# Products of y ahead of the up half of gated block 3, and the rest of M ahead of VectorE's product for up block 2, in a fused delta-rule and gated-MLP kernel

## The chip, the cores and the metric

The kernel runs on one core of one Trainium2 chip. The metric is the device time of one execution in microseconds (us), lower is better. The engines are named as the profile names them: PE is TensorE's matmul, PEld its weight load (which runs beside the matmuls), DVE is VectorE, ACT is ScalarE, POOL is GpSimd, SP is SyncE, which here only issues DMAs.

## The reference, cut to what matters

There are 32 sequences of T = 512 tokens with C = 256 channels. For each of them:

```
x  = x + attn(_layernorm(x))
x  = x + ffn(_layernorm(x))
# attn: layernorm, then delta
#   q, k, v = split(x @ gates_w + gates_b);  k normalised
#   A = tril(k k^T, -1) + I;   u = solve_triangular(A, v)
#   y = (q k^T) (lr * u);      delta = y @ out_w + out_b
#   x = x + delta;   x = x + relu(layernorm(x) @ w1 + b1) @ w2 + b2
# ffn:  h = silu(x @ w_gate^T) * (x @ w_up^T)   (768 hidden);   h @ w_down^T
```

Since q k^T times a matrix can be bracketed the other way, the kernel does not form the 512 x 512 score. It collects one C x C matrix for each sequence, multiplies it by the weights on both sides, and calls the result M. The attention output of the 512 tokens is then one product of the normalised tokens with M. That product is "y" here.

## The kernel before, in words

**Arithmetic.** Most products are made with pairs: an operand is kept as a high part and a rest (`_hi`, `_lo`, tensor type fp32r), and a product is three matmuls (hi by hi, hi by lo, lo by hi; `split_matmul`, L166 to 177). A rest is made by `dve_rest` (L1506), which subtracts the high part, written by ScalarE, from the whole. The gate and up products use the exact integer weights, and so two matmuls (high part and rest of the tokens) for each of the two blocks of 128 channels: four matmuls of 512 columns each for a half of one block.

**Stages.** After a setup phase over all sequences (some 280 us in the profile), a loop over i runs three sequences at once, skewed by one step: the attention part of sequence i (`att`), the MLP and the gate and up halves of sequence i-1 (`mlp`), and the down product of sequence i-2 (`down`). `overlapped` (L988) calls each engine's body with i = 0 to 33. att runs for i = 0 to 31, mlp for i = 1 to 32. Both are there for i = 1 to 31, that is in 31 iterations.

**Order of the work.** Nothing schedules: each engine has its own body, written out by hand (`pe_body` L1155, `act_body` L1341, `dve_body` L1551, `pool_body` L1682, `sp_body` L1782), and runs its instructions in that order. The engines meet only at semaphores (`wait_ge`, and `after`, L984, which waits only when the count is above zero).

**The steps around the change,** in the order of one iteration:

- The gated MLP has six blocks of 128 hidden channels, h = 0 to 5. `pe_gate_up(pe, i, h)` (L1090 to 1111) makes the gate half into PSUM bank FG and then the up half into bank FU (h even) or S0 (h odd). The gate half waits until ScalarE has read the gate half of block h-1 (`sg_ev[h-1]`). The up half waits until VectorE has read the up half of block h-2 (`hf_ev[h-2]`).
- `act_silu` (L1302) makes silu of the gate half. `dve_up` (L1496) multiplies the up half by it and writes hf; it waits for `up_ps`, for `sg_ev[h]`, and for the readers of the buffer of block h-2. `act_hh` (L1311) makes the high part hh of hf, and the rest hl is made on GpSimd (L1733, blocks 0 to 3) or on VectorE (`dve_hl`, L1511, blocks 4 and 5).
- M comes from `pe_square` into bank A1 (L1279). VectorE adds a bias (L1639, `m2`, `m2_sum`), ScalarE makes its high part (L1427, `m_hi` in the profile), VectorE its rest (L1644, `m_lo`, semaphore `m2_ev`).
- PE waits for `m2_ev` and makes y in two halves of two token blocks, into banks A0 and A2 (L1286 to 1289; the rows are `ps<-m_hi,xhT` and `ps<-m_lo,xhT`, line L175), 24 matmuls of 256 columns.
- VectorE adds the tokens to y, one token block at a time (L1657, `a0`), makes the statistics of the layernorm (L1662, L1466, L1471, `ls2`), GpSimd the reciprocal root and the shift (L1680, L1689). Then all three make parts of the normalised tokens xn (the profile calls the tile `work`): VectorE one block (L1556), GpSimd one (L1693), ScalarE two (L1349). These are the first instructions of iteration i+1 on each engine.
- PE transposes xn (`pe_transposes`, L1009, called at L1194, line L1012 in the profile). Between the y products of one iteration and these transposes it has the gate and up halves of blocks 4 and 5, the small products of L1018, and the ten matmuls of L1119 of the down product.
- `dve_invert` (L1542) puts a few steps of a triangular inversion (L208, L212) between the other instructions of VectorE. It is written for 8 sequences at once, and has steps in iterations below 24. The step behind `dve_up(3)` (L1648) is there in 17 of the 31 iterations.

VectorE's order from M on is thus: the bias, `dve_up(2)`, the rest of M, an inversion step, `dve_up(3)`, an inversion step, the four `a0` rows, the statistics, `dve_up(4)`, `dve_up(5)`, `dve_hl(4)`, then the next iteration.

Of the kernel before, what the change touches and what calls it, by code (L numbers as in the profile page):

```python
# [38 lines left out]
A0, A1, A2, S0, FG, FU, FO0, FO1 = range(8)  # L39


def wait(eng, sem, value):

    if isinstance(value, int) and value <= 0:
        return
    eng.wait_ge(sem, value)


def delta_block_kernel(nc, x, dn_g, dn_b, gates_w, gates_b, lr_w, lr_b, out_w, out_b, mn_g, mn_b,
# [31 lines left out]
    with ExitStack() as ctx:  # L81
        def sb(name, shape, dt=F32, c=ctx):
            return c.enter_context(nc.sbuf_tensor(name, shape, dt))
# [3 lines left out]
        def sem(name):  # L87
            held.append(nc.alloc_semaphore(name=name))
            return held[-1]

        def sems(name, n):
            return [sem(f"{name}{k}") for k in range(n)]
# [18 lines left out]
        def pair(name, shape, c=ctx):  # L111

            return sb(name + "_hi", shape, F32R, c=c), sb(name + "_lo", shape, F32R, c=c)
# [7 lines left out]
        wgT = sb("wgT", [P, CB, H], F32R)  # L121
        wuT = sb("wuT", [P, CB, H], F32R)
# [797 lines left out]
        with ExitStack() as mc:  # L920
            def mb(name, shape, dt=F32):
                return sb(name, shape, dt, c=mc)
# [9 lines left out]
            m2 = mb("m2", [P, CB, C])  # L932
            m22 = pair("m2", [P, CB, C], c=mc)
# [25 lines left out]
            m2_ps, m2_sum, m2_hi, m2_ev = sem("m2_ps"), sem("m2_sum"), sem("m2_hi"), sem("m2_ev")  # L959
# [11 lines left out]
            gate_ps, up_ps = sem("gate_ps"), sem("up_ps")  # L971
            sg_ev, hf_ev, hh_ev, hl_ev = sems("sg_ev", HB), sems("hf_ev", HB), sems("hh_ev", HB), sems("hl_ev", HB)
            fo_ps, ot_ev = sems("fo_ps", 2), sems("ot_ev", 2)
# [7 lines left out]
            def blk(j):  # L981
                return slice(j * P, (j + 1) * P)

            def after(eng, sem, n, each=1):  # L984

                wait(eng, sem, min(n, NS) * each)
# [14 lines left out]
            def up_bank(h):  # L1001
                return (FU, S0)[h % 2]
# [4 lines left out]
            with nc.Block() as block:  # L1007
# [65 lines left out]
                def pe_tokens(pe, bank, half, lhs, rhs, done, before=None):  # L1073

                    for q in range(2):
                        mm = split_matmul(pe, ps[:, bank, q * C:(q + 1) * C],
                                          lhs, [(slice(None), k, blk(2 * half + q)) for k in range(CB)],
                                          rhs, [(slice(None), k, slice(None)) for k in range(CB)], True, True,
                                          before=None if q else before)
                    mm.then_inc(done, 1)  # L1080
# [6 lines left out]
                                          xh2T2, [(slice(None), k, slice(None))], k == 0, k == CB - 1)  # L1087
                    mm.then_inc(m1_ps[m], 1)

                def pe_gate_up(pe, i, h):  # L1090

                    if h == 0:
                        after(pe, ot_ev[0], i - 1)
                    else:
                        pe.wait_ge(sg_ev[h - 1], i)
                    for w, bank, done in ((wgT, FG, gate_ps), (wuT, up_bank(h), up_ps)):
                        if bank != FG:
                            if h >= 2:
                                pe.wait_ge(hf_ev[h - 2], i)
                            elif h == 1:  # L1100
                                pe.wait_ge(h1_lo[1], i)
                            else:
                                after(pe, ot_ev[1], i - 1)
                        for k in range(CB):
                            if h == 0 and bank == FG:
                                pe.wait_ge(x3h_ev[k], i)
                                pe.wait_ge(x3l_ev[k], i)
                            for part in (x3h, x3l):
                                mm = pe.matmul(ps[:, bank, :], w[:, k, blk(h)], part[:, k, :],  # L1109
                                               start=(k == 0 and part is x3h), stop=(k == CB - 1 and part is x3l))  # L1110
                        mm.then_inc(done, 1)
# [43 lines left out]
                def pe_body(pe, i, att, mlp, down, m, r):  # L1155
# [112 lines left out]
                    if mlp:  # L1268
                        pe_gate_up(pe, i, 0)
# [5 lines left out]
                    if mlp:  # L1275
                        pe_gate_up(pe, i, 1)
# [4 lines left out]
                        keep_busy(pe, S0, 9)  # L1281
                    if mlp:
                        pe_gate_up(pe, i, 2)
                        pe_gate_up(pe, i, 3)
                    if att:
                        pe.wait_ge(m2_ev, i + 1)  # L1286
                        wait(pe, xhT_in, 16 * i)
                        pe_tokens(pe, A0, 0, xhT2, m22, y_ps[0])
                        pe_tokens(pe, A2, 1, xhT2, m22, y_ps[1])
                    if mlp:  # L1290
                        pe_gate_up(pe, i, 4)
                        pe_gate_up(pe, i, 5)

                @block.tensor
                def _(pe):
                    overlapped(pe_body)(pe)
# [199 lines left out]
                def dve_up(dve, i, h):  # L1496
                    dve.wait_ge(up_ps, HB * i + (h + 1 - HB))
                    dve.wait_ge(sg_ev[h], i)
                    for made in (hh_ev, hl_ev):
                        if h >= 2:  # L1500
                            dve.wait_ge(made[h - 2], i)
                        else:
                            after(dve, made[HB - 2 + h], i - 1)
                    dve.tensor_tensor(hf[:, h % 2, :], ps[:, up_bank(h), :], sg[:, h % 2, :], ALU.mult).then_inc(hf_ev[h], 1)  # L1504

                def dve_rest(dve, lo, whole, hi, hi_done, n_done, done):  # L1506

                    dve.wait_ge(hi_done, n_done)
                    dve.tensor_tensor(lo, whole, hi.bitcast(F32), ALU.subtract).then_inc(done, 1)  # L1509
# [29 lines left out]
                def bank3(bank):  # L1539
                    return ps[:, bank, :].rearrange("p (k c) -> p k c", c=C)  # L1540

                def dve_invert(dve, m, r, first, end):  # L1542

                    if r is not None:
                        for q in range(INV_EACH * r + first, min(INV_EACH * r + end, INV_STEPS + 1)):
                            if q < INV_STEPS:
                                invert_step(dve, lanes, m, q)
                            else:
                                invert_flip(dve, lanes, m, flipped)

                def dve_body(dve, i, att, mlp, down, m, r):  # L1551
# [85 lines left out]
                    if att:  # L1637
                        dve.wait_ge(m2_ps, i + 1)
                        dve.tensor_tensor(m2[:, :, :], bank3(A1), bo_bc[:, :].unsqueeze(1).broadcast_to([P, CB, C]),  # L1639
                                          ALU.add).then_inc(m2_sum, 1)  # L1640
                    if mlp:
                        dve_up(dve, i, 2)
                    if att:
                        dve_rest(dve, m22[1][:, :, :], m2[:, :, :], m22[0][:, :, :], m2_hi, i + 1, m2_ev)  # L1644
                    dve_invert(dve, m, r, 8, 9)
                    if mlp:
                        dve_up(dve, i, 3)
# [23 lines left out]
                @block.vector  # L1671
                def _(dve):
                    dve.memset(p1[:, :, :], 0.0).then_inc(p1_zero, 1)
                    dve.wait_ge(p1_zero, 1)
                    overlapped(dve_body)(dve)
# [152 lines left out]
```

## Time and profile before

| what | value |
|---|---|
| device time, median of 3 runs | 1561.8 us (1560.47 to 1562.3) |
| the profiled execution: its own time | 1562.71 us |
| span of its instructions | 1561.0 us |
| PE busy | 1537.2 us, 98% of the span |
| PEld busy | 1366.3 us, 88% |
| VectorE busy | 1152.4 us, 74% |
| ScalarE busy | 859.0 us, 55% |
| GpSimd busy | 767.8 us, 49% |
| mean granted TensorE clock | 0.999 of full speed |
| chain of waits that ended last | 79% on PE |

In this profile busy time is the union of an engine's instructions. Matmuls overlap in the array and their ends are modelled, so for them the distance between starts tells more than the duration. A number in square brackets behind a row of a timeline is the idle time before it, with what ended it.

### The profile page before, as it was taken

The page shows a single profiled execution, that of the slowest core. Times are in us where ns is not written, and L with a number is a line of the kernel's source. Part 1 is how long each engine was busy: PE and PEld are TensorE (multiplying, and loading weights), DVE is VectorE, ACT ScalarE, POOL GpSimd, SP SyncE. Part 2 cuts the span into 40 slices and gives each one's busy share as a digit, 9 for nine tenths or more (in the row PEclk, how much of TensorE's full clock was granted, in tenths as well). Part 3 has the DMA queues.
Part 4 walks back from the last instruction along what each step waited for, and adds up shares of the span by engine and source line. Part 5 has one row for each costly group of instructions (what it writes and reads, how often), then busy time and mean ns, then how long its engine had stood idle before and what let it go on. Part 6 is the DMA issues. An engine that isn't in the chain of part 4 may idle for free.

```text
span 1561.0 us, 30382 instructions
## 1 busy us (share of the span) xinstructions
PE 1537.2 (98%) x10748; PEld 1366.3 (88%) x10748; DVE 1152.4 (74%) x3071; ACT 859.0 (55%) x1696; POOL 767.8 (49%) x886
## 2 busy tenths in 40 slices
PE   8999998899999999999999999999999999999998
PEld 7999998788888888888888888888888888888887
DVE  6767884578877777788777777887777777777774
ACT  6878774355555555555555555555555555555553
POOL 5446871344444454444444544444444444444442
PEclk9999999999999999999999999999999999999999
DMA  7998997212222322222222222222222222222200
GB/s 243 329 324 300 327 334 258 78 61 75 71 72 74 108 75 75 75 75 75 76 75 101 90 75 75 75 75 75 75 81 96 75 75 75 75 71 77 71 21 28
DMA packets 150168, 178.22 MB, mean 114 GB/s; under 512 B 78850, under 2 KB 132098, under 8 KB 141826
## 3 DMA queue, kind: packets, MB, share of 16 engines
q1 hardware_dynamic: 150018, 176.28, 34.1%
q8 instruction: 87, 1.43, 0.4%
q14 instruction: 63, 0.52, 0.1%
HBM read 98.64 MB, written 77.59 MB: 113 GB/s over the span
## 4 chain that ended last, share of the span: by engine, by line
PE 79%; DVE 2%; ACT 1%; issue 0%; POOL 0%; DVEq 0%; ACTq 0%; POOLq 0%
PE ps L175 34%; PE ps L1109 23%; PE ps L1119 11%; PE ps L1040 4%; PE ps L1012 4%; PE ps L1029 2%; PE ps L1018 1%; PE ps L247 0%; PE ps L1150 0%; DVE work L1556 0%; DVE xh3T_lo L1509 0%; DVE xinv L1454 0%; DVE hl L1509 0%; DVE late L1504 0%; DVE low L199 0%
## 5 line engine op out<-in xcount | busy, mean ns | idle before, releaser
L1733 POOL TENSOR_TENSOR hl<-late,hh 128x512 fp32r<-128x512 f32 x128 | 166.4, 1300 | 209.9 <-ACT hh L1314 209.9
L1309 ACT ACTIVATE late<-ps 128x512 f32<-128x512 f32 x192 | 114.6, 597 | 170.6 <-PE ps L1109 170.6
L1504 DVE TENSOR_TENSOR late<-ps,late 128x512 f32<-128x512 f32 x192 | 132.8, 691 | 95.0 <-PE ps L1109 93.3
L1119 PE MATMUL ps<-wdT,hh 128*128 128x256 f32 x744 | 199.9, 304 | 0.0
L1119 PE MATMUL ps<-wdT,hl 128*128 128x256 f32 x744 | 182.7, 281 | 0.3 <-DVE hl L1509 0.3
L1314 ACT ACTIVATE hh<-late 128x512 fp32r<-128x512 f32 x192 | 121.1, 631 | 108.7 <-DVE late L1504 108.7
L1680 POOL TENSOR_TENSOR sc<-ls,mhalf 128x4 f32<-128x4 f32 x64 | 65.8, 1028 | 221.0 <-DVE ls L1471 221.0
L1109 PE MATMUL ps<-xh3T_hi,wgT 128*128 128x512 f32 x384 | 153.5, 400 | 1.1 <-DVE xh3T_lo L1509 1.1
L1109 PE MATMUL ps<-xh3T_lo,wuT 128*128 128x512 f32 x384 | 152.2, 396 | 0.0
L1109 PE MATMUL ps<-xh3T_lo,wgT 128*128 128x512 f32 x384 | 151.9, 396 | 0.0
L1109 PE MATMUL ps<-xh3T_hi,wuT 128*128 128x512 f32 x384 | 151.5, 395 | 0.0
L1119 PEld LDWEIGHTS ps<-wdT,hh 128*128 128x128 f32 x744 | 140.4, 189 | 3.4 <-ACT late L1331 0.4
L1119 PEld LDWEIGHTS ps<-wdT,hl 128*128 128x128 f32 x744 | 140.5, 189 | 2.1 <-DVE hl L1509 0.5
L1318 ACT ACTIVATE z_hi<-ps 128x256 fp32r<-128x256 f32 x128 | 49.0, 383 | 163.1 <-PE ps L1040 163.1
L175 PE MATMUL ps<-pT,xhTk 128*128 128x258 f32 (+2 forms) x768 | 119.6, 305 | 2.5 <-ACT scal L509 2.5
L1715 POOL TENSOR_TENSOR xhm_lo<-xh,xhm_hi 128x1024 fp32r<-128x1024 f32 x32 | 76.7, 2398 | 80.2 <-ACT xhm_hi L1385 80.2
L175 PEld LDWEIGHTS ps<-pT,xhTk 128*128 128x128 f32 x768 | 108.1, 191 | 2.7 <-ACT scal L509 2.7
L1454 DVE COPY xinv<-ps 32x64 f32<-32x64 f32 (+2 forms) x384 | 84.8, 221 | 30.8 <-PE ps L1029 25.9
L1706 POOL TENSOR_TENSOR work<-xa,a 128x1024 f32<-128x1024 f32 x32 | 76.7, 2396 | 44.7 <-DVE hl L1509 41.5
L1724 POOL TENSOR_TENSOR xa<-xt,b_bc 128x1024 f32<-128x1024 f32 x32 | 76.7, 2397 | 43.9 <-DVE work L1487 43.9
L175 PE MATMUL ps<-m_hi,xhT 128*128 128x256 f32 x512 | 96.0, 281 | 0.2 <-DVE m_lo L1509 0.2
L1109 PEld LDWEIGHTS ps<-xh3T_hi,wgT 128*128 128x128 f32 x384 | 72.1, 188 | 26.8 <-ACT late L1309 12.7
(219 smaller groups left out, 4743.1 us busy)
## 6 DMA issues: line engine op xcount, KB each, us to landing
xhT_scratch<-xhTk SPq DMA_DIRECT2D x32, 1024.0 KB, 7.0
xhT<-xhT_scratch SPq DMA_DIRECT2D x32, 1024.0 KB, 6.4
gg_scratch<-late SPq DMA_DIRECT2D x32, 640.0 KB, 4.3
gg<-gg_scratch SPq DMA_DIRECT2D x32, 640.0 KB, 4.0
xk<-in_L_attn_x_dram SPq DMA_DIRECT2D x32, 512.0 KB, 5.6
xt<-in_L_attn_x_dram SPq DMA_DIRECT2D x32, 512.0 KB, 4.1
out_dram<-late SPq DMA_DIRECT2D x31, 512.0 KB, 2.9
low_scratch<-late SPq DMA_DIRECT2D x128, 16.0 KB, 3.1
```

Source lines behind the costliest of these rows:

```text
L175: mm = pe.matmul(dst, a[ka], b[kb], start=start, stop=(stop and n == 0), **kw)
L1109: mm = pe.matmul(ps[:, bank, :], w[:, k, blk(h)], part[:, k, :], start=(k == 0 and part is x3h), stop=(k == CB - 1 and part is x3l))
L1119: mm = pe.matmul(ps[:, (FG, FU)[j // 2], (j % 2) * C:(j % 2 + 1) * C], part[:, h, blk(j)], wdT[:, h, :], start=(h == 0 and part is hh), st ...
L1309: act.activation(sg[:, h % 2, :], ps[:, FG, :], ACT.Silu, scale=QUANT).then_inc(sg_ev[h], 1)
L1314: act.activation(hh[:, h, :], hf[:, h % 2, :], ACT.Copy).then_inc(hh_ev[h], 1)
L1454: op = dve.tensor_copy(xinv[rows, j, 0:f * SUB], ps[j * SUB:(j + 1) * SUB, row_bank(f), 0:f * SUB])
L1504: dve.tensor_tensor(hf[:, h % 2, :], ps[:, up_bank(h), :], sg[:, h % 2, :], ALU.mult).then_inc(hf_ev[h], 1)
L1680: pool.tensor_tensor(sc[:, 0, :], ls[:, 0, :], mhalf4[:, :], ALU.pow).then_inc(done, 1)
L1706: pool.tensor_tensor(xa2[:, :, :], xa[:, :, :], a0[:, :, :], ALU.add).then_inc(xa_done, 1)
L1715: pool.tensor_tensor(xhm2[1][:, :, :], xh[:, :, :], xhm2[0][:, :, :].bitcast(F32), ALU.subtract).then_inc(xhm_lo, 1)
L1724: pool.tensor_tensor(xa[:, :, :], xt[:, :, :], b2_bc[:, :].unsqueeze(1).broadcast_to([P, TB, C]), ALU.add).then_inc(xb_done, 1)
L1733: pool.tensor_tensor(hl[:, h, :], hf[:, h % 2, :], hh[:, h, :].bitcast(F32), ALU.subtract).then_inc(hl_ev[h], 1)
```

## The change

The up half of block 3 is split off from `pe_gate_up(pe, i, 3)` and is issued after the products of y. The rest of M is issued ahead of `dve_up(dve, i, 2)` on VectorE. The rest of VectorE's order is as it was, and so are the orders of ScalarE, GpSimd and SyncE.

```diff
-                def pe_gate_up(pe, i, h):
-
-                    if h == 0:
-                        after(pe, ot_ev[0], i - 1)
-                    else:
-                        pe.wait_ge(sg_ev[h - 1], i)
-                    for w, bank, done in ((wgT, FG, gate_ps), (wuT, up_bank(h), up_ps)):
+                def pe_gate_up(pe, i, h, which=(0, 1)):
+
+                    if 0 in which:
+                        if h == 0:
+                            after(pe, ot_ev[0], i - 1)
+                        else:
+                            pe.wait_ge(sg_ev[h - 1], i)
+                    for q in which:
+                        w, bank, done = ((wgT, FG, gate_ps), (wuT, up_bank(h), up_ps))[q]
                         if bank != FG:
                             if h >= 2:
                                 pe.wait_ge(hf_ev[h - 2], i)
...
                     if mlp:
                         pe_gate_up(pe, i, 2)
-                        pe_gate_up(pe, i, 3)
+                        pe_gate_up(pe, i, 3, (0,))
                     if att:
                         pe.wait_ge(m2_ev, i + 1)
                         wait(pe, xhT_in, 16 * i)
                         pe_tokens(pe, A0, 0, xhT2, m22, y_ps[0])
                         pe_tokens(pe, A2, 1, xhT2, m22, y_ps[1])
                     if mlp:
+                        pe_gate_up(pe, i, 3, (1,))
                         pe_gate_up(pe, i, 4)
                         pe_gate_up(pe, i, 5)
...
+                    if att:
+                        dve_rest(dve, m22[1][:, :, :], m2[:, :, :], m22[0][:, :, :], m2_hi, i + 1, m2_ev)
                     if mlp:
                         dve_up(dve, i, 2)
-                    if att:
-                        dve_rest(dve, m22[1][:, :, :], m2[:, :, :], m22[0][:, :, :], m2_hi, i + 1, m2_ev)
                     dve_invert(dve, m, r, 8, 9)
                     if mlp:
                         dve_up(dve, i, 3)
```

## Rows read from the trace of the kernel before

**Rows 1.** The page's first part: busy us, share of the span, instructions.
```profile
PE 1537.2 (98%) x10748; PEld 1366.3 (88%) x10748; DVE 1152.4 (74%) x3071; ACT 859.0 (55%) x1696; POOL 767.8 (49%) x886
```

**Rows 2.** Groups by form, 300 to 1520 us, L1012: busy, mean ns | idle before.
```profile
L1012 PE MATMUL ps<-ident,work 128*128 128x128 f32 x496 | 65.9, 276 | 2.0 <-DVE work L1556 1.8 <-issue 0.2
...
L1012 PEld LDWEIGHTS ps<-ident,work 128*128 128x128 f32 x496 | 54.9, 140 | 11.6 <-DVE work L1556 7.7
```

**Rows 3.** Timeline of PE, one iteration, block 3 to block 4 (start, us).
```profile
923.29 0.39 PE L1109 MATMUL ps<-xh3T_hi,wuT 128*128 128x512 f32 x1
...
923.99 0.39 PE L1109 MATMUL ps<-xh3T_lo,wuT 128*128 128x512 f32 x1
924.22 0.28 PE L175 MATMUL ps<-m_hi,xhT 128*128 128x256 f32 x1
...
927.05 0.39 PE L1109 MATMUL ps<-xh3T_hi,wgT 128*128 128x512 f32 x1
```

**Rows 4.** Timeline of ScalarE, same iteration.
```profile
922.09 0.62 ACT L1427 ACTIVATE m_hi<-m 128x512 fp32r<-128x512 f32 x1
...
931.48 1.10 ACT L1349 ACTIVATE work<-a,sc 128x256 f32<-128x256 f32 x2 [0.18 <-POOL sc L1689]
```

**Rows 5.** Timeline of VectorE, same iteration, up block 2 to xn.
```profile
922.53 0.69 DVE L1504 TENSOR_TENSOR late<-ps,late 128x512 f32<-128x512 f32 x1 [1.17 <-PE ps L1109]
923.13 0.69 DVE L1509 TENSOR_TENSOR m_lo<-m,m_hi 128x512 fp32r<-128x512 f32 x1
...
924.47 0.69 DVE L1504 TENSOR_TENSOR late<-ps,late 128x512 f32<-128x512 f32 x1 [0.46 <-PE ps L1109]
925.07 0.32 DVE L212 TENSOR_TENSOR inv<-inv,tmp 128x112 f32<-128x112 f32 x1
925.93 0.87 DVE L1657 SCALAR_TENSOR_TENSOR a<-xt,scal,ps 128x256 f32<-128x256 f32 x2 [0.54 <-PE ps L175]
927.25 0.88 DVE L1657 SCALAR_TENSOR_TENSOR a<-xt,scal,ps 128x256 f32<-128x256 f32 x2 [0.45 <-PE ps L175]
928.04 1.40 DVE L1662 BATCH_NORM_STATS2 bs<-a 128x6 f32<-128x256 f32 x4
...
929.76 0.17 DVE L1471 TENSOR_SCALAR ls<-mv 128x4 f32<-128x4 f32 x1
...
931.61 0.68 DVE L1509 TENSOR_TENSOR hl<-late,hh 128x512 fp32r<-128x512 f32 x1
932.20 0.58 DVE L1556 TENSOR_SCALAR work<-a,mv,sc 128x256 f32<-128x256 f32 x1
```

**Rows 6.** Timeline of GpSimd, same iteration.
```profile
930.01 1.01 POOL L1680 TENSOR_TENSOR sc<-ls,mhalf 128x4 f32<-128x4 f32 x1 [2.81 <-DVE ls L1471]
...
931.56 1.07 POOL L1693 TENSOR_SCALAR work<-a,sc 128x256 f32<-128x256 f32 x1 [0.20 <-POOL sc L1689]
```

**Rows 7.** Timeline of the weight loads, same iteration, at the transposes.
```profile
932.84 0.86 PEld L1012 LDWEIGHTS ps<-ident,work 128*128 128x128 f32 x8 [0.19 <-DVE work L1556]
```

**Rows 8.** Timelines of VectorE and PE, the iteration that begins at 575.
```profile
576.05 1.47 DVE L1556 TENSOR_SCALAR work<-a,mv,sc 128x256 f32<-128x256 f32 x1
...
577.58 1.09 PE L1012 MATMUL ps<-ident,work 128*128 128x128 f32 x8 [0.87 <-DVE work L1556]
```

**Rows 9.** Timeline of all engines, iteration 0, M to y and the xn of GpSimd.
```profile
290.36 0.63 ACT L1427 ACTIVATE m_hi<-m 128x512 fp32r<-128x512 f32 x1 [3.22 <-DVE m L1639]
...
291.77 0.39 PE L175 MATMUL ps<-m_hi,xhT 128*128 128x256 f32 x1 [0.17 <-DVE m_lo L1509]
...
292.00 0.28 PE L175 MATMUL ps<-m_lo,xhT 128*128 128x256 f32 x1
...
299.36 0.56 POOL L1693 TENSOR_SCALAR work<-a,sc 128x256 f32<-128x256 f32 x1
```

**Rows 10.** Timeline of PE at its longest stall in the loop's start.
```profile
299.71 0.27 PE L1029 MATMUL ps<-xinv,p 128*32 128x32 f32 x8 [1.90 <-DVE p L1446]
```

**Rows 11.** Table by stretches: PE, PEld, DVE, ACT, POOL busy, PEclk, DMA share, GB/s.
```profile
298.00:300.00 2.00, 0.29 (x9) 0.25 (x9) 0.87 (x2) 0.65 (x2) 1.75 (x4) 1.00 1.11 407
```

## The prediction

> **What bounds the kernel now.** I read the engines' busy times first. PE is busy for 98% of the span and VectorE for 74% [rows 1]. So there is next to no idle time of PE to win back, and what can change the time is a new one. Then I read the groups of the loop for a place where PE already waits. It is the transposes of xn: eight matmuls in each iteration, 496 in that stretch, whose weight loads stand idle for 11.6 us in all, 7.7 of them put down to VectorE's part of xn [rows 2]. In the single iteration the load begins at 932.84, 0.19 us after it could have [rows 7], and VectorE's instruction had ended at 932.20 + 0.58 = 932.78 [rows 5]. So the chain from y to xn is already the last to arrive there, by a hair. How PE answers to a later one is seen in an iteration in which it is late by itself: there the same VectorE instruction takes 1.47 us and not 0.58, 0.89 more, and PE shows an idle time of 0.87 [rows 8]. **A delay of the chain from y to xn is paid in full.**
>
> The chain goes by the program's order on VectorE. The first half of y lets it start the a0 rows at 925.93, after 0.54 us of waiting. The second half lets it go on at 927.25, after 0.45 us. Statistics begin at 928.04 and the variance is out at 929.76 [rows 5]. GpSimd follows at 930.01 and 931.56, ScalarE at 931.48 [rows 4, 6].
>
> **The change, part by part.**
>
> *Nothing is added or removed.* The same instructions run, so no engine's busy time should move. The moved PE step is four matmuls and their loads, and the moved VectorE step one instruction. No DMA is moved past anything. SyncE's load of the next tokens waits for the last a0 row, and moves with it.
>
> *The rest of M goes first on VectorE.* Before, VectorE took up block 2 at 922.53 and the rest of M at 923.13 [rows 5]. ScalarE's high part begins at 922.09 [rows 4], behind its silu of block 2, and the change leaves that alone. Iteration 0 shows what follows it when VectorE and PE stand ready: from the high part's start at 290.36 to the first y matmul at 291.77 are 1.41 us [rows 9]. So y can begin at 922.09 + 1.41 = 923.50. PE is free for it at 923.29, where the up half of block 3 began [rows 3]. That is a stall of 0.21 us, which the order before did not have. Restarting costs 0.11 more: behind the wait the second matmul of iteration 0 comes 0.23 us after the first [rows 9], where the 24 of the steady iteration take 2.83 us [rows 3], 0.12 each. The product of up block 2 comes out 0.8 us later on VectorE. Who waits for it is ScalarE (its high part, then silu of block 3) and PE's up half of block 4; both are now needed only behind y and the up half of block 3. I cost that at nothing. If the cover were gone it would be those 0.8 us.
>
> *y goes ahead of the up half of block 3.* y takes 927.05 - 924.22 = 2.83 us [rows 3]. With the stall it ends at 923.50 + 0.11 + 2.83 = 926.44, and the up half of block 3 has that as its start. Its last matmul begins 0.70 us on (923.99 - 923.29) [rows 3], at 927.14. VectorE took the product 0.48 us behind that start (924.47 - 923.99) [rows 3, 5], so now at 927.62, where before it was 924.47.
>
> *What is queued behind that wait.* VectorE's product of up block 3 still stands ahead of the a0 rows. PE delivers y first, but VectorE stands waiting for the other product. All four a0 rows are queued behind it. The product holds the engine for 0.60 us (925.07 - 924.47), so the rows start at 928.22 if no inversion step stands between. They then run without waits, 0.79 us a pair (928.04 - 927.25) [rows 5], 1.58 in all, and the statistics begin at 929.80. Before it was 928.04. **The chain is 1.76 us later.** In 17 iterations there is the inversion step as well, which used to lie in VectorE's wait for y and now stands in the chain: 0.32 us [rows 5], so 2.08.
>
> *From the statistics to the transposes.* Nothing on this way has room to give much back. The up products of blocks 4 and 5 stood behind the statistics before, and still do. GpSimd's root waits for the variance [rows 6]. Only the end has a little room. GpSimd's part of xn took 1.07 us [rows 6] beside VectorE's rest of block 4 at 931.61 [rows 5], and 0.56 in iteration 0 [rows 9], where nothing of that kind ran beside it. VectorE now takes the product of up block 5 straight behind that of block 4, without its wait for PE, so that the rest of block 4 comes a little earlier against GpSimd's part and they meet less. But ScalarE's two blocks end at 931.48 + 1.10 = 932.58 [rows 4], 0.20 us before the 932.78 of VectorE, and stay there. The gain here is thus between 0 and 0.20 us, and I take 0.10. The GPSIMD Engine Reference of the Trainium skill (Specifications) says that GpSimd shares its SBUF interfaces with VectorE and is held up by VectorE instructions with two SBUF inputs or in a two-port mode. By that rule the meeting shrinks and the whole 0.20 is won; by a fixed 1.07 us for GpSimd's part nothing is. The rows lean to the rule.
>
> *The other new waits on PE.* ScalarE's silu of block 4 stands behind the high part of block 3, which now comes 3.15 us later with its product. PE may stall a few tenths of a us ahead of the gate half of block 5. That stall and the 0.32 us of the later y lie ahead of the transposes, where PE waits for xn anyhow, so they are no terms of their own.
>
> **The sum.** 31 iterations x 1.76 = 54.6; 17 x 0.32 = 5.4; less 31 x 0.10 = 3.1. That is 56.9 us on the profiled execution's own time of 1562.7, thus 1619.6. That execution lies 0.9 above the median of the runs, so against the median it is **1619 us**, 3.6% slower. The bounds of the terms: without the stall and restart ahead of y (0.32) and with the whole 0.20 won at the end, the stall is 1.24 us and the time 1561.8 + 38.4 + 5.4 = 1606. With both the stall and no gain at the end it is 1561.8 + 60.0 = 1622, and if the stalls ahead of the transposes were not covered either, some 0.3 us each time, 1631.
>
> **The rivals.**
>
> *Faster: the earlier y gives earlier transposes.* y begins 924.22 - 923.50 = 0.72 us sooner. If the a0 rows could start with it, the transposes would no longer wait: 31 x 0.19 [rows 7] = 5.9 us less, and 1556 us. It decides on whether VectorE has passed the product of up block 3 when the first half of y is there. For it: VectorE did wait for y before, 0.54 us [rows 5]. Against it: PE makes that product's operand only after the whole of y, and VectorE's order has it first. I see no way round that. Chance 0.02.
>
> *No change: the chain has slack that I do not see.* The delay would have to be absorbed between the statistics and the transposes. Against it stand the 0.87 us of PE idle behind a late xn [rows 8]. A part might be absorbed, if other instructions that are late today move under the new wait. With half of the delay lost in this way it is 1562 + 28 = 1590. Chance 0.06 for such a part, and 0.03 for all of it (1562 us).
>
> *A dearer stall: TensorE's clock falls.* The new stall is 1.7 us long. At a stall of 1.90 us [rows 10] the granted clock of that stretch stayed at 1.00 [rows 11], which is the 2.4 GHz level, and PE was busy there for just 0.29 of 2.00 us. No row of this trace shows the 1.2 GHz level. If each stall brought it for as long as it lasts itself, PE would do half the work in another 1.7 us, which adds 0.85 x 31 = 26 us, and 1645 us. Chance 0.03. The page TensorE: Matmul & The Clock Gate (HAM oscillation) warns that idle gaps between matmul bursts can put the clock back to its lower level. That speaks against this change, and the stall of rows 10 did not set it off.
>
> *The stalls ahead of the transposes add up,* 1631 us as above. Chance 0.05. The remaining 0.81 is for the forecast.
>
> **How the numbers follow.** The forecast's own bounds are 1606 to 1622. I widen them for the durations, each read in one iteration, where an error of 0.3 us in the stall makes 9 us, and up to the case of the added stalls: 1601 to 1634. What lies outside is the part absorbed, no change, faster, and the fallen clock, together 0.14. The least change that a measurement of this kernel can tell from none is about 0.2%, 3 us. Faster by more has 0.02, within it 0.03, slower by more 0.95.
>
> **What the changed profile would show.** Right: an idle time of VectorE of some 3 us ahead of the product of up block 3, put down to PE, and none ahead of the a0 rows; the statistics some 3.5 us behind the last y matmul's start where it was 1.1; PE idle for 1.5 to 2.0 us at the transposes in 31 iterations, put down to the makers of xn; each iteration 1.6 to 2.0 us longer. PE's instructions and durations are as before and its share falls to about 95%. Wrong: if PE's idle time lies mainly at the y products, my account of the late M is too small. If the transposes start without a wait, the chain had slack. If the matmuls' spacing grows behind the stall, it is the clock.

## The result, and the profile after

The changed kernel takes **1615.0 us** (median of 4 runs, 1613.3 to 1616.4), against 1562.05 for the kernel before. The ratio is 1.034, with a 95% interval of 1.032 to 1.036. The forecast was 1619 us with a range of 1601 to 1634. The profiled execution took 1614.7 us, 52.0 more than that of before.

The page's first part of the changed kernel (busy us, share of the span, instructions) answers to [rows 1]:

```profile
PE 1566.8 (97%) x10748; PEld 1368.3 (85%) x10748; DVE 1140.6 (71%) x3071; ACT 854.5 (53%) x1696; POOL 765.1 (47%) x886
```

No instruction was added, and yet PE is "busy" for 29.6 us more. Its row is a union of matmuls whose ends are modelled, so that a wait of a few tenths lies under the tail of the matmul ahead of it. The distance between starts shows it. VectorE's busy time fell by 11.8 us; the last section says why.

The timeline of VectorE in the changed kernel, in the iteration that answers to [rows 5] (the same inversion step, 128x112):

```profile
947.66 0.69 DVE L1512 TENSOR_TENSOR m_lo<-m,m_hi 128x512 fp32r<-128x512 f32 x1 [1.39 <-ACT m_hi L1430]
948.27 0.68 DVE L1507 TENSOR_TENSOR late<-ps,late 128x512 f32<-128x512 f32 x1
...
952.48 0.69 DVE L1507 TENSOR_TENSOR late<-ps,late 128x512 f32<-128x512 f32 x1 [3.35 <-PE ps L1111]
953.09 0.26 DVE L212 TENSOR_TENSOR inv<-inv,tmp 128x112 f32<-128x112 f32 x1
953.27 1.65 DVE L1660 SCALAR_TENSOR_TENSOR a<-xt,scal,ps 128x256 f32<-128x256 f32 x4
954.84 1.40 DVE L1665 BATCH_NORM_STATS2 bs<-a 128x6 f32<-128x256 f32 x4
...
956.55 0.17 DVE L1474 TENSOR_SCALAR ls<-mv 128x4 f32<-128x4 f32 x1
```

This is where the time goes on VectorE: 3.35 us of waiting ahead of the product of up block 3, put down to PE, and behind it four a0 rows in one piece that wait for nothing. Before, they came in two pairs with a wait ahead of each [rows 5].

The timeline of PE in the same iteration answers to [rows 3, 7]:

```profile
945.38 0.39 PE L1111 MATMUL ps<-xh3T_hi,wgT 128*128 128x512 f32 x1
...
947.97 0.40 PE L1111 MATMUL ps<-xh3T_lo,wgT 128*128 128x512 f32 x1
948.41 0.38 PE L175 MATMUL ps<-m_hi,xhT 128*128 128x256 f32 x1
948.63 0.28 PE L175 MATMUL ps<-m_lo,xhT 128*128 128x256 f32 x1
...
951.35 0.39 PE L1111 MATMUL ps<-xh3T_hi,wuT 128*128 128x512 f32 x1
...
953.91 0.40 PE L1111 MATMUL ps<-xh3T_lo,wuT 128*128 128x512 f32 x1
954.37 0.50 PE L1111 MATMUL ps<-xh3T_hi,wgT 128*128 128x512 f32 x1
954.71 0.40 PE L1111 MATMUL ps<-xh3T_lo,wgT 128*128 128x512 f32 x1
...
958.14 0.38 PE L1121 MATMUL ps<-wdT,hh 128*128 128x256 f32 x1
958.87 0.39 PE L1121 MATMUL ps<-wdT,hl 128*128 128x256 f32 x1 [0.34 <-DVE hl L1512]
959.57 1.07 PE L1012 MATMUL ps<-ident,work 128*128 128x128 f32 x8 [0.31 <-POOL work L1696]
```

The columns in square brackets show just 0.65 us of idle time. The starts show 1.84: in the kernel before a matmul of 512 columns is followed after 0.23 us, one of 256 after 0.12, and the transposes start 0.26 behind the last matmul of the down product. What exceeds these is lost. Ahead of y it is 0.21, and 0.11 more behind its first matmul. Ahead of the gate half of block 5 (954.37) it is 0.23 and 0.11. Ahead of the last two matmuls of L1121, which need the high part and the rest of block 4, it is 0.13 and 0.61. Ahead of the transposes it is 0.44.

Between the starts of L1018 in consecutive iterations, the changed kernel takes 1.55 to 1.63 us more in the iterations without inversion steps and 1.74 to 1.98 more in most of those with them. In the two iterations in which a GpSimd memset delayed xn before, it takes only 0.67 and 0.68 more. Together that is 50.7 of the 52.0 us; the loop's spacing is the loss.

### The profile page after: what moved, and what is told of

Its sections match the earlier page's. It is cut to its first block, busy times and chain, and to the rows that moved or that the text cites. A ratio compares the mean times of both kernels' runs of the same rounds, so it can differ in the third digit from the quotient of the medians.

```text
span 1612.9 us, 30382 instructions
## 1 busy us (share of the span) xinstructions
PE 1566.8 (97%) x10748; PEld 1368.3 (85%) x10748; DVE 1140.6 (71%) x3071; ACT 854.5 (53%) x1696; POOL 765.1 (47%) x886
## 4 chain that ended last, share of the span: by engine, by line
PE 65%; DVE 9%; POOL 5%; issue 2%; ACT 2%; POOLq 0%; DVEq 0%; ACTq 0%
PE ps L175 33%; PE ps L1111 13%; PE ps L1121 9%; PE ps L1040 4%; PE ps L1012 4%; DVE a L1660 3%; DVE bs L1665 3%; POOL sc L1683 2%; POOL work L1696 2%; PE ps L1029 1%; DVE m_lo L1512 1%; ACT late L1312 1%; DVE mv L1469 1%; ACT m_hi L1430 1%; PE ps L247 0%
## 5 line engine op out<-in xcount | busy, mean ns | idle before, releaser
L1507 DVE TENSOR_TENSOR late<-ps,late 128x512 f32<-128x512 f32 x192 | 129.5, 688 | 136.5 <-PE ps L1111 134.8
L1121 PE MATMUL ps<-wdT,hh 128*128 128x256 f32 x744 | 203.1, 307 | 1.5 <-ACT hh L1317 0.5
L1121 PE MATMUL ps<-wdT,hl 128*128 128x256 f32 x744 | 187.1, 285 | 10.6 <-DVE hl L1512 10.6
L1111 PE MATMUL ps<-xh3T_hi,wgT 128*128 128x512 f32 x384 | 156.2, 407 | 3.0 <-DVE xh3T_lo L1512 1.1
L1121 PEld LDWEIGHTS ps<-wdT,hl 128*128 128x128 f32 x744 | 140.4, 189 | 18.4 <-DVE hl L1512 16.7
L1111 PE MATMUL ps<-xh3T_lo,wgT 128*128 128x512 f32 x384 | 152.1, 396 | 0.0
L1111 PE MATMUL ps<-xh3T_lo,wuT 128*128 128x512 f32 x384 | 151.8, 395 | 0.0
L1111 PE MATMUL ps<-xh3T_hi,wuT 128*128 128x512 f32 x384 | 151.7, 395 | 0.0
L1121 PEld LDWEIGHTS ps<-wdT,hh 128*128 128x128 f32 x744 | 140.3, 189 | 8.4 <-ACT hh L1317 4.8
L1111 PEld LDWEIGHTS ps<-xh3T_hi,wgT 128*128 128x128 f32 x384 | 72.1, 188 | 38.2 <-ACT late L1312 22.4
L175 PE MATMUL ps<-m_hi,xhT 128*128 128x256 f32 x512 | 99.3, 287 | 1.5 <-DVE m_lo L1512 0.2
```

Of the source, the lines that this page charges most:

```text
L175: mm = pe.matmul(dst, a[ka], b[kb], start=start, stop=(stop and n == 0), **kw)
L1121: mm = pe.matmul(ps[:, (FG, FU)[j // 2], (j % 2) * C:(j % 2 + 1) * C], part[:, h, blk(j)], wdT[:, h, :], start=(h == 0 and part is hh), st ...
```

## The experiments

Labels name the runs. Each was compared with the kernel before, run on the same chip. Times are medians.

**e2, PE's part alone.** On the changed kernel:

```diff
-                    if att:
+                    if mlp:
+                        dve_up(dve, i, 2)
+                    if att:
                         dve_rest(dve, m22[1][:, :, :], m2[:, :, :], m22[0][:, :, :], m2_hi, i + 1, m2_ev)
-                    if mlp:
-                        dve_up(dve, i, 2)
```

> PE's part of the change alone: y ahead of the up half of block 3, while VectorE keeps the rest of M behind the product of up block 2. Theory 1: the rest of M ends 0.37 us later than in the changed kernel, so y, the up half of block 3, its product and the a0 rows are all 0.37 us later, 31 x 0.37 = 11.5 us on top of 1615: 1626 us. Rival, the time at which y begins does not count since VectorE is behind anyhow: 1615 us.

Measured: 1628.1 us against 1563.1, ratio 1.041 (1.040 to 1.043). Theory 1 holds, to 2 us. Most iterations are 0.3 to 0.4 us longer than in the changed kernel. The loads of y waited longer: the first row is that of the changed kernel, the second that of e2, each from the waits of the weight loads (us in total, times, longest).

```profile
PEld ps L175 <- DVE m_lo L1512: 15.2, 32, 0.5
```

```profile
PEld ps L175 <- DVE m_lo L1512: 27.1, 32, 0.9
```

So the start of y counts, although VectorE is behind: y has the up half of block 3 behind it, and that product is what the a0 rows stand behind.

**e3, VectorE's part alone,** the same two lines exchanged in the kernel before, PE's order unchanged.

> VectorE's part of the change alone: the rest of M ahead of the product of up block 2, PE in the order before. Theory 1: the product of up block 2 is 0.8 us later, ScalarE's silu of block 3 and with it VectorE's product of up block 3 are some 0.75 us later, which VectorE's waits for y (0.54 and 0.45 us) nearly take up: 1562 us, at most 1566. Rival, the late product of up block 2 is part of the loss: 31 x 0.75 = 23 us, 1585 us.

Measured: 1562.6 us against 1563.1, ratio 0.9997 (0.9987 to 1.0006). No effect, as theory 1 had it. Two rows of VectorE's timeline show that the room in its waits took up the later start:

```profile
925.33 0.86 DVE L1657 SCALAR_TENSOR_TENSOR a<-xt,scal,ps 128x256 f32<-128x256 f32 x2
926.47 0.87 DVE L1657 SCALAR_TENSOR_TENSOR a<-xt,scal,ps 128x256 f32<-128x256 f32 x2 [0.27 <-PE ps L175]
```

The wait of 0.54 us ahead of the first pair is gone, the second pair still waits for y. The loss belongs to PE's part, together with VectorE's order behind it; the other part makes it some 12 us smaller (65.0 us of loss in e2, 53.0 in the changed kernel, each against its own measurement of the kernel before).

**e4b, the chain delayed by itself.** The kernel before, with

```diff
+            bsx, more = mb("bsx", [P, 2, 6]), sem("more")
...
+                        for j in range(2):
+                            dve.wait_ge(a0_ev[j], i + 1)
+                            wait(dve, more, 2 * i + j)
+                            dve.bn_stats(bsx[:, j, :], a0[:, j, :]).then_inc(more, 1)
                         for j in range(TB):
                             dve.wait_ge(a0_ev[j], i + 1)
```

> The kernel before, with two of the four statistics of the a0 rows computed a second time into a spare tile: 2 x 0.33 us of VectorE's work more in the chain from y to xn, some 0.66 to 0.85 with the waits between them, nothing else. Theory 1, a delay of that chain is paid in full by PE: 31 x 0.66 to 0.85, less up to 0.1 each time at its end: 1579 to 1588 us. Rival, the chain has slack at the transposes: 1562 to 1570 us.

Measured: 1588.0 us against 1562.8, ratio 1.016 (1.015 to 1.018). VectorE's timeline gives the dose, 938.89 - 938.02 = 0.87 us ahead of the statistics proper:

```profile
938.02 0.95 DVE L1664 BATCH_NORM_STATS2 bsx<-a 128x6 f32<-128x256 f32 x2
938.89 1.39 DVE L1667 BATCH_NORM_STATS2 bs<-a 128x6 f32<-128x256 f32 x4
```

The iterations without a memset are 0.71 to 0.87 us longer, 0.79 as a rule (the first is an exception, at 2.18). That is nine tenths of the dose. The chain from y to xn has next to no slack, under 0.1 us: **the assumption on which the forecast stood is shown here apart from the change.** The two iterations with the memset are 0.1 us shorter.

**e1, the a0 rows ahead of the product.** The changed kernel, with

```diff
-                    if mlp:
-                        dve_up(dve, i, 3)
-                    dve_invert(dve, m, r, 9, INV_EACH)
                     if att:
                         wait(dve, xin, i * 16)
...
                                                      op0=ALU.mult, op1=ALU.add).then_inc(a0_ev[j], 1)
+                    if mlp:
+                        dve_up(dve, i, 3)
+                    dve_invert(dve, m, r, 9, INV_EACH)
+                    if att:
                         for j in range(TB):
                             dve.wait_ge(a0_ev[j], i + 1)
```

> The changed kernel, with VectorE's product of up block 3 (and the inversion step behind it) moved behind the four a0 rows. Theory 1, the a0 rows pay for standing behind that product: they now start when y is there, the product still comes at the same time, and the statistics begin some 0.1 to 0.4 us later than before the change instead of 1.9. What is left are PE's own two waits, 0.32 us ahead of y and 0.33 ahead of the gate half of block 5, no longer covered but for 0.19: 31 x 0.46 = 14 us, so 1576 us. Theory 2, these two waits are covered here too: 1562 + 31 x 0.13 + 17 x 0.3 = 1571 us or less. Rival, the loss comes from the y products' place on PE and not from VectorE's order: it stays near 1615 us.

Measured: 1580.0 us against 1563.1, ratio 1.010 (1.009 to 1.012). So about 36 of the 53 us go when four rows change places with one product. What is left is nearest to theory 1 (1576) and speaks against theory 2 (1571 or less). The timeline of VectorE:

```profile
932.44 0.87 DVE L1657 SCALAR_TENSOR_TENSOR a<-xt,scal,ps 128x256 f32<-128x256 f32 x2 [1.09 <-PE ps L175]
933.77 0.87 DVE L1657 SCALAR_TENSOR_TENSOR a<-xt,scal,ps 128x256 f32<-128x256 f32 x2 [0.45 <-PE ps L175]
934.70 0.69 DVE L1507 TENSOR_TENSOR late<-ps,late 128x512 f32<-128x512 f32 x1
```

The gate half of block 5 began at 936.59, as in the row below from the weight loads, 1.89 us behind the product at 934.70. In the changed kernel it was 954.37 - 952.48 = 1.89 as well.

```profile
936.59 0.19 PEld L1111 LDWEIGHTS ps<-xh3T_hi,wgT 128*128 128x128 f32 x1 [0.50 <-ACT late L1312]
```

What is left in e1 is PE's own lateness and not the chain from y. VectorE's part of xn ends at 940.09 + 0.40 = 940.49, and the transposes start at 940.54. It stands behind the product of up block 5, and that product waited for PE, 0.65 us where it was 0.37 before the change:

```profile
938.76 0.69 DVE L1507 TENSOR_TENSOR late<-ps,late 128x512 f32<-128x512 f32 x1 [0.65 <-PE ps L1111]
940.09 0.40 DVE L1559 TENSOR_SCALAR work<-a,mv,sc 128x256 f32<-128x256 f32 x1
```

**e5 and e6, the statistics by halves.** In e5 the kernel before, in e6 that of e1, gets

```diff
                                                      op0=ALU.mult, op1=ALU.add).then_inc(a0_ev[j], 1)
-                        for j in range(TB):
+                            if j == 1:
+                                for t in range(2):
+                                    dve.wait_ge(a0_ev[t], i + 1)
+                                    dve.bn_stats(bs2[:, t, :], a0[:, t, :]).then_inc(bn2[t], 1)
+                        for j in range(2, TB):
```

(in e6 the last line comes behind the product of up block 3).

> The kernel before, with the statistics of the first two a0 rows computed while VectorE waits for the second half of y: the variance is out some 0.4 us earlier. Theory 1: PE is late at the transposes by just 0.19 us, so no more than that comes back: 31 x 0.19 = 5.9 us, 1557 us. Rival A, PE does not lose those 0.19 us at all since its matmuls in the array cover them: 1563 us, no change. Rival B, all 0.4 us come back: 1551 us.

> The kernel of e1, with the statistics of the first two a0 rows between the two pairs of rows, and so ahead of the product of up block 3. The chain to xn is then some 0.5 us earlier than in e1 and earlier than before the change. Theory 1, what is left in e1 are PE's own waits ahead of y and ahead of the gate half of block 5, and not the chain: no change against e1, 1577 to 1580 us. Rival, the chain still ends last in e1: some 8 to 12 us less, 1570 us.

Measured, e5: **1555.2 us** against 1562.8, ratio 0.9948 (0.9936 to 0.9961). It is the fastest version in this study. Most iterations are 0.15 to 0.2 us shorter and the two with the memset 1.07, in sum 7.6 us: the number of theory 1, with 2 x 0.9 us on top that it had left out. The way to it was another. VectorE's part of xn does not start earlier (11.77 us behind the gate half of block 2, which began at 913.15; it was 11.73), since it stands behind the product of up block 5, which waits for PE. It got shorter, 0.41 us and not 0.58, because GpSimd's part of xn is now over before it starts:

```profile
923.72 0.69 DVE L1504 TENSOR_TENSOR late<-ps,late 128x512 f32<-128x512 f32 x1 [0.90 <-PE ps L1109]
924.92 0.41 DVE L1556 TENSOR_SCALAR work<-a,mv,sc 128x256 f32<-128x256 f32 x1
```

```profile
923.74 0.56 POOL L1697 TENSOR_SCALAR work<-a,sc 128x256 f32<-128x256 f32 x1 [0.20 <-POOL sc L1693]
```

Measured, e6: 1577.7 us against 1562.8, ratio 1.010 (1.008 to 1.011). The time is as theory 1 has it, but e6 is no test of it, since the chain did not get earlier. VectorE's instruction behind the variance (L1474) starts 0.64 us sooner than in e1 and takes 0.89 us instead of 0.24. GpSimd's root starts 9.93 us behind the gate half of block 2, in e1 9.92: it stands behind GpSimd's own rest of block 3, which the late product of up block 3 had pushed back.

```profile
935.00 0.89 DVE L1474 TENSOR_SCALAR ls<-mv 128x4 f32<-128x4 f32 x1
```

```profile
934.58 1.28 POOL L1741 TENSOR_TENSOR hl<-late,hh 128x512 fp32r<-128x512 f32 x1 [2.93 <-ACT hh L1317]
935.97 1.01 POOL L1688 TENSOR_TENSOR sc<-ls,mhalf 128x4 f32<-128x4 f32 x1
```

What speaks for theory 1 in e1 and e6 is the wait of the product of up block 5 for PE, shown for e1 above (0.66 us in e6).

**e7, no wait at y.** e6, with two of the four matmuls of up block 3 ahead of y (`pe_gate_up` takes the numbers of the blocks of 128 channels as a further argument, and signals behind the second):

```diff
                         pe_gate_up(pe, i, 3, (0,))
+                        pe_gate_up(pe, i, 3, (1,), (0,))
...
-                        pe_gate_up(pe, i, 3, (1,))
+                        pe_gate_up(pe, i, 3, (1,), (1,))
```

> The kernel of e6, with two of the four matmuls of the up half of block 3 (the first 128 channels) back ahead of y and the other two behind it. PE then has 0.47 us of work in the 0.21 us in which it waits for the rest of M, and no restart. Theory 1, what e6 still loses are PE's own two waits: the one ahead of y goes, 31 x 0.32 = 10 us less, 1568 us, and the 0.33 ahead of the gate half of block 5 stays. Rival, the two waits are one and the same loss, and what goes here comes back at block 5 or at the transposes: 1578 us.

Measured: 1581.5 us against 1563.7, ratio 1.012 (1.010 to 1.013). My theory was wrong and the rival right: the wait at y is gone and came back at block 5. PE's waits for it stand on the page of waits as 15.5 us in 31 times:

```profile
PE ps L1111 <- ACT late L1314: 15.5, 31, 0.5
```

The two timelines say why. The second pair of a0 rows and the product behind it on VectorE, and the gate half of block 5 on PE:

```profile
896.80 0.86 DVE L1659 SCALAR_TENSOR_TENSOR a<-xt,scal,ps 128x256 f32<-128x256 f32 x2
897.58 0.69 DVE L1509 TENSOR_TENSOR late<-ps,late 128x512 f32<-128x512 f32 x1
```

```profile
899.47 0.50 PE L1111 MATMUL ps<-xh3T_hi,wgT 128*128 128x512 f32 x1 [0.50 <-ACT late L1314]
```

PE had started the last matmul of that product at 896.71, and VectorE needs some 0.45 us from there, but it was at the rows until 897.58, and again the gate half came 1.89 us behind. The product had a fixed place behind y's second half and two rows, so an earlier operand was of no use, and y itself began 0.27 us later than in e6 (3.30 us behind the gate half of block 2, not 3.03).

**e8 and e9, ScalarE's silu of block 4 ahead of its high part of block 3,** in the kernels of e6 and e7:

```diff
-                        act_hh(act, i, 3)
                         act_silu(act, i, 4)
+                        act_hh(act, i, 3)
```

> The kernel of e6, with ScalarE's silu of block 4 ahead of its high part of block 3. Theory 3: in e1, e6 and e7 the time is set by one row of releases, VectorE's product of up block 3, ScalarE's high part of it, its silu of block 4, and then PE's gate half of block 5, which starts 1.89 us behind the product in all of them. Here the last two let go of the product, so PE's wait of 0.23 us and its restart go. But the rest of block 3 on GpSimd is some 0.7 us later and stands ahead of its reciprocal root, so that xn is out some 12.7 us behind the gate half of block 2 where it was 12.2 before the change: the transposes are 0.4 us late, and with the inversion's iterations 1572 to 1576 us. Rival, the wait at block 5 is not what sets the time: 1578 us, as e6.

> The kernel of e7, with ScalarE's silu of block 4 ahead of its high part of block 3. Theory 3: e7 has no wait at y any more and 0.66 us of it at the gate half of block 5, so that all of its loss lies there. With silu 4 ahead that goes. xn, by way of the later rest of block 3 on GpSimd, is out about 12.4 us behind the gate half of block 2, where the transposes started before the change: 1562 to 1567 us. Rival, the loss of e7 lies elsewhere: 1581 us.

Measured: e8 1596.5 us, ratio 1.022 (1.021 to 1.023); e9 1579.6, ratio 1.011 (1.009 to 1.012). Both missed. The releases that I named were right: the loads of L1111 wait for the silus as little as before the change (12.8 and 13.0 us in all, where e6 had 22.3). But the whole loss reappeared at the transposes. The waits of PE, e8 first:

```profile
PE ps L1012 <- POOL work L1701: 27.5, 30, 1.2
```

```profile
PE ps L1012 <- POOL work L1703: 7.6, 24, 0.4
PE ps L1012 <- ACT work L1354: 2.8, 7, 0.6
```

In e8 GpSimd's root began 10.5 us behind the gate half of block 2, and its part of xn ended at 13.0, where I had expected xn at 12.7. But I had followed GpSimd's part alone. ScalarE's two blocks start behind the same root and take 1.10 us, GpSimd's only 0.56 when nothing disturbs it, and so ScalarE's end last, at 13.4, and the transposes start at 13.6. (The row above puts that wait down to GpSimd's part, which was over by then.) In e9 the root began at 10.3, 0.8 us later than before the change, again behind GpSimd's own rest of block 3. The parts of GpSimd and ScalarE ended at 12.9, where I had expected 12.4.

## Why the prediction was right

It was right in sign, size and mechanism: the queue behind VectorE's wait delays xn, and PE pays. It was off in where PE would be seen waiting, and it had misread which part of xn the delay reaches. Point by point:

*The start of y.* To lay the two iterations over each other I count from the first matmul of the gate half of block 2, which is 945.38 in the changed kernel and in the one before, from PE's timeline,

```profile
920.47 0.39 PE L1109 MATMUL ps<-xh3T_hi,wgT 128*128 128x512 f32 x1
```

The forecast was 923.50 - 920.47 = 3.03 us behind it, measured 948.41 - 945.38 = 3.03, and the restart at 0.22 between the first two matmuls. The 1.41 us read in iteration 0 were the right price. e2 priced that start a second time.

*The wait on VectorE.* Forecast for the product 3.15 us later than before; in the frame of that gate half it is 952.48 - 945.38 = 7.10 us, where 7.15 was forecast. The row of four a0 rows took 1.57 us to the statistics, forecast 1.58. The inversion step cost 0.18 us there, not 0.32: the row's duration was 0.32, but the next instruction starts before it ends. **For an engine that runs back to back, the price is the distance between starts.** The steps are of different widths. Over the 17 iterations they cost 0.15 to 0.33 us, 0.26 on average, so the term of 5.4 us was 4.4. That it came out near is in part luck: one duration, read too long, stood for steps of which the widest cost as much.

*The end of the chain.* The variance came 1.88 us later against that gate half, the transposes 1.82. I had taken 0.10 to be won between them, and 0.06 were. By the rule on GpSimd's shared interfaces, from the page GPSIMD Engine Reference (Specifications) of the Trainium skill, I had worked out 0.20. The trace agrees with the rule itself (1.05 to 1.08 us for GpSimd's part beside VectorE's rest of block 4, which has two SBUF inputs, and 0.56 in e5 beside a product that reads PSUM), but the two instructions still met: VectorE's rest of block 4 at 958.12 and GpSimd's part of xn right behind it at 958.35. It went from 1.07 us [rows 6] to 1.05.

```profile
958.35 1.05 POOL L1696 TENSOR_SCALAR work<-a,sc 128x256 f32<-128x256 f32 x1 [0.20 <-POOL sc L1692]
```

*Which part of xn.* I had called the chain from y the last to arrive because VectorE's part of xn ended last, at 932.78. That reading was wrong. VectorE's part stood behind the product of up block 5, and what that waited for was PE, not the variance:

```profile
931.00 0.69 DVE L1504 TENSOR_TENSOR late<-ps,late 128x512 f32<-128x512 f32 x1 [0.37 <-PE ps L1109]
```

In the changed kernel this wait is gone, and VectorE's part ends 2.59 us behind the start of the row that adds a constant to the variance (956.55), where it was 3.02 (929.76). The delay came through the other two parts, which start as soon as GpSimd's root and shift are there. Before, GpSimd's ended at 932.63 and ScalarE's at 932.58, just 0.15 and 0.20 us ahead of VectorE's. Now GpSimd's ends last, at 959.40, and PE starts 0.17 us behind it, where it had started 0.06 behind VectorE's. So this way had some 0.04 us of slack. That all three parts ended within 0.20 us of each other is why the delay was paid nearly in full. The PE idle time of 0.87 us in [rows 8] could not show it, since there VectorE's part itself was longer; e4b does. In this the forecast had some luck.

*The sum.* 56.9 us were forecast, the medians give 53.0. Per iteration without inversion it was 1.66 and measured 1.55 to 1.63. The largest part of the difference is one thing that I had in front of me: VectorE's xn of 1.47 us in [rows 8] was not late by itself. It stood beside a GpSimd memset, and that happens in two of the 31 iterations. With the new order VectorE's part is through before the memset begins, and those two lost only 0.7 us each. That is 2 us. Another 1.0 us is the inversion steps, as above, and the rest is a stall that was shorter by 0.03 to 0.11 us in each iteration.

*Where PE waits.* I expected 1.5 to 2.0 us at the transposes and a PE share of 95%. Of the 1.84 us only 0.44 lie there; 1.40 lie ahead, at y, at the gate half of block 5 and at the rest of block 4, which is VectorE's work behind the same statistics. I had called the first two covered, and they were: a wait earlier on PE just leaves less at the transposes. In e1, where the cover is gone, the loss is 0.53 to 0.64 us in most iterations (0.46 expected). "No engine's busy time should move" was wrong for PE, for the reason given above.

*The rivals.* "Faster" and "no slack seen" are out by e4b: a delay of 0.87 us cost 0.79. "The stalls add up" is out, since the total is that of the chain. The clock: the mean granted clock is 0.999 as before, that of the loop from 310 us on is 1.00, and matmuls behind the new waits are spaced as ever (0.23 us at 954.71 to 954.94). The page TensorE: Matmul & The Clock Gate (HAM oscillation) of the Trainium skill warns of idle gaps; waits of 0.1 to 0.6 us, spread over 14 us, did not set that off here. But two things that I wrote of the clock were wrong. The trace of the kernel before does have a stretch at half the clock, the 1.2 GHz level, in the setup phase, after PE had stood idle for 2.48 us. And in the changed kernel the stall of 1.90 us that answers to [rows 10] ends at 298.31, and the clock is at 0.50 from 300 to 302 us, so that stall is no proof that the clock holds. Whether it brought the lower clock is not shown; before the change it did not [rows 11]. Two rows by stretches, before and changed, columns as in [rows 11]:

```profile
258.00:260.00 2.00, 2.00 (x10) 2.00 (x9) 0.00 (x0) 0.00 (x0) 0.00 (x0) 0.50 0.47 139
```

```profile
300.00:302.00 2.00, 2.00 (x10) 2.00 (x11) 0.88 (x4) 0.00 (x0) 0.82 (x1) 0.50 0.51 83
```

Both lie outside the steady loop, in which the 53 us are lost.

**What can't be said.** No version in which y goes first came near the kernel before. Each moved the loss: to the a0 rows (the change), to block 5 (e1, e6, e7), to the transposes (e8, e9). All of these change where the product of up block 3 or its high part stands. In e1 and in e6 to e9 GpSimd's root stood right behind GpSimd's own rest of block 3, and in no run was that rest moved behind the root. Whether some order of all four engines would make an early y pay was not settled. The e5 run says what there is to win at the transposes: 0.15 to 0.2 us in most iterations.

## What to carry to other kernels

When a step is moved ahead of another on one engine, read the consumers' order too: an engine that runs its list in order gains nothing from an operand that comes early if it waits first for the one that was moved back. Price such a change by the whole queue behind that wait, and check whether the end of the queue has slack where the bound engine meets it. And look for the waits already there: doing half of the later work in them (the statistics by halves) gave 7.6 us here, with no step moved between engines. Last, ask of the instruction that ends last what it waited for itself. Here it was VectorE's part of xn, and it waited for PE by way of another product, not for the chain that I had in mind.

## What the runs showed of the hardware that I had not expected

VectorE and GpSimd hold each other up in small instructions, at times by more than their own length. The memset in the kernel before, beside VectorE's instruction of [rows 8], from GpSimd's timeline:

```profile
576.43 0.95 POOL L184 MEMSET inv<- 128x1024 f32 x1
```

VectorE's instruction began at 576.05, took 1.47 us and ended at 577.52, 0.14 after the memset's end. The same operation takes 0.41 us where VectorE is through first, as in the changed kernel beside its own memset:

```profile
917.21 0.41 DVE L1559 TENSOR_SCALAR work<-a,mv,sc 128x256 f32<-128x256 f32 x1
```

```profile
917.82 0.95 POOL L184 MEMSET inv<- 128x1024 f32 x1
```

The mean of this operation was 638 ns before and 406 in the changed kernel, which is 7 us of the 11.8 by which VectorE's busy time fell. The other way round, GpSimd's part of xn took 1082 ns on average before, beside VectorE's rest of block 4. In e5 it runs beside VectorE's product of up block 5, which reads PSUM, and takes 556 (groups by form, busy and mean ns):

```profile
L1697 POOL TENSOR_SCALAR work<-a,sc 128x256 f32<-128x256 f32 x30 | 16.7, 556 | 6.1 <-POOL sc L1693 6.1
```

And in e6 an instruction of 4 elements for each partition (the variance plus a constant) took 541 ns on average instead of 163. The average is over the two layernorms of an iteration. Only the one of this chain stands beside GpSimd's rest of block 3, and it takes 0.73 to 1.08 us:

```profile
L1474 DVE TENSOR_SCALAR ls<-mv 128x4 f32<-128x4 f32 x60 | 32.5, 541 | 1.0
```

With it, what e6 had won by its earlier statistics was gone. It did not cost time of its own here, since the root on GpSimd stood behind that same rest of block 3.
